# Two stages in one block with loads for the second under the first, and a basis summed on POOL, in a three-stage token mixer

## The chip, the cores and the metric

The kernel runs on one core of one Trainium2 chip. The core has five engines with instruction streams of their own: TensorE (PE in the profile; its weight loads are listed as PEld), VectorE (DVE), ScalarE (ACT), GpSimd (POOL), and SyncE (SP), which here only issues DMA transfers. The engines wait for each other through semaphores. The metric is the device time of one execution in microseconds (us), as the median of three runs.

## What is computed

The input x holds, for 16 batches, a complex 192 x 64 table. The reference makes three steps of it. The first, cut to what matters here:

```python
dtA = A * dt[:, None]
C = C * (jnp.exp(dtA) - 1.0) / A
ell = jnp.arange(L, dtype=jnp.float32)              # L = 512
V = jnp.exp(dtA[:, :, None] * ell)
K = 2.0 * jnp.einsum('chn,hnl->chl', C, V).real     # (16, 192, 512): 16 sequences of 192 rows
```

The second adds a retention layer to it: layernorm, projections q, k (512 wide), v and g (1024 wide), a rotary embedding on q and k, scores with a decay per head, an RMS norm of each head's output, a gate, and an output projection:

```python
scores = jnp.einsum('bihd,bjhd->bhij', q * scale, k) * D[None]
o = jnp.einsum('bhij,bjhd->bihd', scores, v)
o = o * rms * g_norm_weight
o = o * (g * jax.nn.sigmoid(g))
return o.reshape(B, T, H * DV) @ Wo
```

The third adds a causal softmax attention with 16 heads, whose keys and values are picked by a top-1 gate. The change does not touch the work of that step.

## The kernel before

The program is three blocks, one after the other: `block_p` (units), `block_q` (retention) and `block_f` (attention). Each block writes its rows to device memory (`h_tok`, `qk`, `v`, `g`, then `h2`), the next one reads them. At the end of a block all engines wait for each other and for the last stores, and only then does the next block begin.

**Units.** The 192 rows are cut into 24 units of 8 rows x 16 batches = 128 tokens. For each unit the first step's exponential is built from products of smaller tables. DVE makes two products, `pc` (real part of one digit times real part of the other) and `qs` (the imaginary counterparts), each 128 x 1024 (`build`, L523 and L525). POOL makes the moving operand `m` (`moving`, L644, L645, L650). TensorE's `spectrum` then adds the two products inside the matrix engine: for each of the 8 rows it runs one matmul with `pc` and one with `qs` as weights, both 64 columns wide, into the same accumulator (L698, L699), 16 matmuls in a unit.

After `spectrum(u+2)` a unit's rows are transposed to rows of tokens (`row_transposes`, L707), copied out by ACT (`h_evac`), their statistics taken (DVE L533, L536; POOL `scales`, L659 to L662), normalised (ACT L363), transposed back (`x_transposes`, L715), and split into a high and a low part (ACT `x_high` L370, DVE `x_low` L541). Six projections of 12 matmuls of 512 columns each follow (`project`, L724: q, k, v0, v1, g0, g1).

What stands in which slot is written out by hand in each engine's `slot(u)`. On TensorE slot u is: projection q of unit u, row transposes of u+1, projection k, spectrum of u+2, projections v0 and v1, transposes of x of u+1, projections g0 and g1. On POOL it is: `decay` (even u, L616), `scales(u+1)`, two `rope_add(u)` (L669), `corners` (every other unit, L626 to L632) and `moving(u+3)`. On DVE an even slot also holds `reduce` (L454 to L461) and `scale` (L512, L513) of the chunk two units on; ACT's part of that chunk is `trigonometry`. SP stores g of unit u-1, `h_tok` of u+1, and q/k and v of unit u (all L272).

In the first slots the six weight blocks are loaded through a buffer `stage` and split into `wr_high` (ACT `w_copy`, L313) and `wr_low` (DVE `split_weights`, L443), between the first units' work.

**Retention.** It goes over 8 pairs of batches of 384 tokens, in three tiles of 128 rows; tile 0 comes from units 0 to 15, the other tiles also need the last unit. SP's queue first loads q/k of pair 0 (`load_qk(0, t)`, L846 to L851, 1.5 MB), constants, v and g of pair 0 (1.5 MB each), the output weights `wo_raw` (2 MB), then q/k and v of pair 1. TensorE transposes q and k of pair 0 (L1098), computes the first scores (L1114), then transposes q and k of pair 1's tile 0 and runs the first `values` (L1130), in that order. ACT makes `wo_high` (L985) and DVE makes `wo_low` (`split_weights`, L1058, two instructions); on DVE these stand ahead of the first score masks (`masked`, L1002). In each slot DVE alternates masks with `gate_o` (L1013), which waits for POOL's norm (L1078 to L1081).

## Time and profile before

| what | value |
|---|---|
| median of three runs | 1482.92 us (1481.59 to 1484.98) |
| the profiled execution's own time | 1483.9 us |
| its span, first to last instruction | 1482.1 us |
| TensorE busy | 1322.8 us (89%), 8504 matmul records |
| DVE, ACT, POOL busy | 816.1, 595.5, 452.5 us |
| mean granted TensorE clock | 0.958 of full speed |

All rows shown are of that profiled execution. A row of the timeline gives the start, the time, the engine, the line, the operation with its tiles, how many instructions were merged into the row (x), and in brackets how long the engine had been idle before and who released it. A matmul of two f32 tiles is recorded as two instructions. Matmuls overlap in their records, so their spacing is read from the starts, not from the durations.

### The profile page before, as it was taken

What the parts mean: (1) busy time and instruction counts of PE and PEld (TensorE: products, weight loads), DVE (VectorE), ACT (ScalarE), POOL (GpSimd) and SP (SyncE); (2) the same over time, 40 slices, a digit from 0 to 9 for tenths busy, and PEclk for the clock granted to TensorE, in tenths of its full rate; (3) what the DMA queues carried; (4) which work ended last, traced back from release to release, by engine and by line L of the source; (5) the groups of instructions that cost most, each with busy time, mean ns of one, the idle gap of its engine ahead of it and who ended that gap; (6) DMA issues with size and microseconds to landing.
All of it is one profiled execution on the core that took longest, in us unless ns stands there. A gap on an engine that the chain in (4) does not pass through costs nothing. (4 is left out here: it accounts for less than half of the span.)

```text
span 1482.1 us, 23784 instructions
## 1 busy us (share of the span) xinstructions
PE 1322.8 (89%) x8504; PEld 1109.5 (75%) x8504; DVE 816.1 (55%) x1629; ACT 595.5 (40%) x1777; POOL 452.5 (31%) x696
## 2 busy tenths in 40 slices
PE   0799999999999995599999998489899998999997
PEld 0678888888888884478888886368788787878775
DVE  8656656655566321455555552345666656566566
ACT  3443333333334221333333321234546556454646
POOL 3555445544554310233333231021221203122121
PEclk9999999999999997799999999599999999999999
DMA  3222222222222225856655411354141423514040
GB/s 147 98 87 93 93 105 88 93 93 100 86 93 93 93 90 177 241 164 171 171 162 162 147 43 44 141 107 93 37 100 36 93 70 62 116 40 101 16 93 30
DMA packets 59525, 150.71 MB, mean 102 GB/s; under 512 B 7696, under 2 KB 24336, under 8 KB 57872
## 3 DMA queue, kind: packets, MB, share of 16 engines
q1 hardware_dynamic: 59408, 149.18, 34.0%
q8 instruction: 69, 1.13, 0.3%
q14 instruction: 48, 0.39, 0.1%
HBM read 67.37 MB, written 56.62 MB: 84 GB/s over the span
## 5 line engine op out<-in xcount | busy, mean ns | idle before, releaser
L724 PE MATMUL psum<-wr_high,x_high 128*128 128x512 f32 x576 | 234.1, 406 | 5.0 <-DVE x_low L541 5.0
L724 PE MATMUL psum<-wr_high,x_low 128*128 128x512 f32 x576 | 228.9, 397 | 0.0
L724 PE MATMUL psum<-wr_low,x_high 128*128 128x512 f32 x576 | 228.3, 396 | 0.0
L1466 ACT ACTIVATE probs<-psum,row_max 128x256 f32<-128x256 f32 (+1 forms) x384 | 165.1, 453 | 107.6 <-issue 75.2
L1716 POOL TENSOR_TENSOR picked_rows<-picked_rows 128x768 f32<-128x768 f32 (+1 forms) x64 | 61.0, 953 | 269.6 <-DVE picked_rows L1600 265.8
L724 PEld LDWEIGHTS psum<-wr_high,x_high 128*128 128x128 f32 x576 | 109.0, 189 | 28.6 <-DVE x_low L541 5.8
L724 PEld LDWEIGHTS psum<-wr_high,x_low 128*128 128x128 f32 x576 | 108.7, 189 | 25.9
L1618 DVE TENSOR_REDUCE row_max<-psum 128x2 f32<-128x512 f32 (+1 forms) x160 | 109.5, 684 | 31.8 <-PE psum L1821 31.8
L724 PEld LDWEIGHTS psum<-wr_low,x_high 128*128 128x128 f32 x576 | 109.1, 189 | 23.4
L937 ACT ACTIVATE square_scratch<-psum 128x128 f32<-128x128 f32 x192 | 50.7, 274 | 185.4 <-PE psum L1130 185.4
L698 PE MATMUL psum<-m,basis 128*128 128x64 f32 x384 | 76.8, 283 | 40.8 <-POOL m L650 40.8
L1013 DVE SCALAR_TENSOR_TENSOR gate_rows_q<-psum,rr,gate_rows_q 128x128 f32<-128x128 f32 x192 | 55.3, 344 | 91.7 <-POOL rr L1081 91.7
L1821 PE MATMUL psum<-k_stack_t,q_stack_t 128*128 128x256 f32 (+1 forms) x384 | 103.2, 365 | 0.0
L1832 PE MATMUL psum<-ident,probs 128*128 128x128 f32 x640 | 100.6, 281 | 1.5 <-ACT probs L1466 1.4
L698 PEld LDWEIGHTS psum<-m,basis 128*128 128x128 f32 x384 | 63.7, 203 | 42.7 <-issue 40.8
L1130 PEld LDWEIGHTS psum<-v_rows,s_t 128*128 128x128 f32 x640 | 81.2, 195 | 18.2 <-DVE s_t L1002 14.3
L1130 PE MATMUL psum<-v_rows,s_t 128*128 128x128 f32 x640 | 85.5, 282 | 9.3 <-DVE s_t L1002 9.3
L561 DVE SCALAR_TENSOR_TENSOR gate_rows<-gate_rows,psum 128x512 f32<-128x512 f32 x48 | 33.0, 687 | 102.4 <-ACT gate_rows L389 102.4
L1002 DVE SCALAR_TENSOR_TENSOR s_t<-psum,consts_r 128x256 f32<-128x256 f32 (+1 forms) x192 | 72.1, 432 | 25.7 <-PE psum L1114 25.7
L669 POOL TENSOR_TENSOR stage<-stage 128x512 f32<-128x512 f32 x48 | 81.0, 1701 | 14.9 <-DVE stage L556 14.9
L1832 PEld LDWEIGHTS psum<-ident,probs 128*128 128x128 f32 x640 | 77.6, 144 | 10.1 <-ACT probs L1466 2.4
L1466 ACT ACTIVATION_READ_ACCUMULATOR probs<-psum,row_max 128x1 f32 x384 | 84.5, 220 | 0.0
(200 smaller groups left out, 3027.5 us busy)
## 6 DMA issues: line engine op xcount, KB each, us to landing
qk<-stage SPq DMA_DIRECT2D x24, 512.0 KB, 2.6
v<-stage SPq DMA_DIRECT2D x24, 512.0 KB, 2.6
g<-gate_rows SPq DMA_DIRECT2D x24, 512.0 KB, 2.6
q_stack_t<-q_t_high SPq DMA_DIRECT2D x64, 192.0 KB, 4.2
q_stack_t<-q_t_low SPq DMA_DIRECT2D x64, 192.0 KB, 5.8
qk_rows<-qk SPq DMA_DIRECT2D x16, 512.0 KB, 5.5
v_rows<-v SPq DMA_DIRECT2D x16, 512.0 KB, 6.9
gate_rows_q<-g SPq DMA_DIRECT2D x16, 512.0 KB, 8.9
```

What stands on the lines that cost most here:

```text
L669: G.tensor_tensor(rqk[:, n], rt[:, n, 0], rt[:, n, 1], ALU.add).then_inc(rope_rows.sem, 1)
L698: nc.tensor.matmul(out, pc[:, f, h].rearrange("p x y -> p (x y)"), rhs, start=True, stop=False)
L724: last = nc.tensor.matmul(psum[:, PB[(6 * u[1] + n) % 4], :], x[:, q, k], ww[:, w, k, :], start=c == 0, stop=c == 3 * KC - 1)
L937: last = nc.scalar.activation(sqs[:, h % 2, t], psum[:, OB[h % 2], t * RV:(t + 1) * RV], ACT.Square, accum_out=ss[:, h % 2, t:t + 1])
L1002: last = V.scalar_tensor_tensor(st[:, h % 2, c], s_block(h, b), gk[:, kt, h:h + 1], mask[:, c], ALU.mult, ALU.mult)
L1013: last = V.scalar_tensor_tensor(y, psum[:, OB[h % 2], t * RV:(t + 1) * RV], rr[:, h % 2, 3, t:t + 1], y, ALU.mult, ALU.mult)
L1130: last = nc.tensor.matmul(psum[:, OB[h % 2], qt * RV:(qt + 1) * RV], st[:, h % 2, b * P:(b + 1) * P], v[:, i % 2, kt, hv], start=first, st ...
L1466: last = nc.scalar.activation(pr[:, g % 2, c], psum[:, SB[g % 3], c], ACT.Exp, scale=SCALE_F, bias=mx[:, g % 3, 1, x:x + 1], accum_out=dsu ...
L1618: V.reduce_max(mx[:, g % 3, 0, 0:nh], psum[:, SB[g % 3], :].rearrange("p (h n) -> p h n", h=nh), AX).then_inc(s_max.sem, 1)
L1716: return G.tensor_tensor(sel[:, x, :, 0:n], sel[:, x, :, 0:n], sel[:, x, :, n:2 * n], ALU.add)
L1821: last = mm(bank[:, x * nb * P:(x + 1) * nb * P], qsT[:, i % 2, h, t * P:(t + 1) * P], ksT[:, i % 2, k0:k0 + nb * P], start=False, stop=x ...
L1832: last = nc.tensor.transpose(psum[:, PTB[g % 2], x * P:(x + 1) * P], pr[:, g % 2, x * P:(x + 1) * P], ident[:, :])
```

## The change

There are four edits.

1. **Basis sum on POOL.** POOL gets a new step `basis_add(u)` at the end of its slot, after `moving(u+3)`: it waits for DVE's two products and adds `qs` to `pc`, one instruction over 128 x 1024. `spectrum` waits for it (semaphore `basis_summed`) and runs 8 matmuls instead of 16.
2. **One block.** Units and retention share one block: each engine goes from its last slot of the units into retention. Retention's buffers are laid over those of the units, so single waits on the last unit (`last_unit`) stand where one of its buffers or accumulators is reused.
3. **First loads under the last unit.** SP issues, in the last unit's slot and ahead of that unit's q/k and v stores, tile 0 of q/k, v and g of pair 0, the constants and `wo_raw` (`prefetch`). The other tiles of pair 0 follow when the stores that they need have landed.
4. **Weight split later.** DVE's two `split_weights` of the output projection stand in retention's slot 0 after the gates of heads 2 and 4, instead of ahead of the first mask. The accumulator banks of retention get other numbers.

```diff
+    def prefetch(sp):
+
+        for s in (*qk_in, *v_in, *g_in, *h_in, *stored):
+            s.prime(sp)
+        units["filtered"](sp)
+        load_qk(sp, 0, 0)
+        load_v(sp, 0, 0)
+        load_g(sp, 0, 0)
+        sp.dma_start(cr[:, :], d["consts_r"]).then_inc(const_in, 16)
+        sp.dma_start(gnorm_t[:, 0:1], d["g_norm"]).then_inc(const_in, 16)
+        for n in range(NW):
+            sp.dma_start(raw[:, n], d["w_f"][n].rearrange("p k f -> p (k f)")).then_inc(w_in[n], 16)
...
+        def basis_add(u):
+            f = u[1] % 2
+            pool.wait_ge(v_ready.sem, v_ready.of(u, 1))
+            flat = lambda x: x.rearrange("p h y x -> p (h y x)")
+            G.tensor_tensor(flat(pc[:, f]), flat(pc[:, f]), flat(qs[:, f]), ALU.add).then_inc(basis_sum.sem, 1)
...
             def spectrum(u):
                 f = u[1] % 2
-                pe.wait_ge(v_ready.sem, v_ready.of(u, 1))
+            pe.wait_ge(basis_sum.sem, basis_sum.of(u, 1))
...
-                    nc.tensor.matmul(out, pc[:, f, h].rearrange("p x y -> p (x y)"), rhs, start=True, stop=False)
-                    last = nc.tensor.matmul(out, qs[:, f, h].rearrange("p x y -> p (x y)"), rhs, start=False, stop=True)
+                last = nc.tensor.matmul(out, pc[:, f, h].rearrange("p x y -> p (x y)"), rhs, start=True, stop=True)
...
-            for t in range(NT):
-                load_qk(0, t)
-            sp.dma_start(cr[:, :], d["consts_r"]).then_inc(const_in, 16)
...
-            load_v(0)
-            load_g(0)
...
+        units["qk_stored"](sp)
+        load_qk(sp, 0, 1)
+        load_qk(sp, 0, 2)
+        units["v_stored"](sp)
+        load_v(sp, 0, 1)
+        load_v(sp, 0, 2)
+        units["g_stored"](sp)
+        load_g(sp, 0, 1)
+        load_g(sp, 0, 2)
+        units["h_stored"](sp)
...
+                elif m < HG - 1:
+                    split_weights(m - 1)
```

How the instructions stand now is shown at three places. The first is POOL in an odd slot of the units, before: the norm scales' last step, the two rope sums, the moving operand, and the next slot's scales.

```order
L662 TENSOR_TENSOR rs_p<-rs_p 128x1 [waits pool_chain_n]
L669 TENSOR_TENSOR stage<-stage 128x512 [waits qk_stored,rope_products]
L669 TENSOR_TENSOR stage<-stage 128x512 [waits rope_products]
L644 TENSOR_TENSOR mt<-cin,xy 128x512 [waits m_ready]
L645 TENSOR_TENSOR mt<-cin,xy 128x512
L650 TENSOR_TENSOR m<-mt 128x512 [waits k_summed,m_chain]
L659 TENSOR_TENSOR rs_p<-mv_p,small_p 128x1 [waits x_rows_normed,mean_var]
```

And the same place of the changed kernel:

```order
L682 TENSOR_TENSOR stage<-stage 128x512 [waits qk_stored,rope_products]
L682 TENSOR_TENSOR stage<-stage 128x512 [waits rope_products]
L651 TENSOR_TENSOR mt<-cin,xy 128x512 [waits m_ready]
L652 TENSOR_TENSOR mt<-cin,xy 128x512
L657 TENSOR_TENSOR m<-mt 128x512 [waits k_summed,m_chain]
L663 TENSOR_TENSOR basis<-basis 128x1024 [waits basis_products]
L672 TENSOR_TENSOR rs_p<-mv_p,small_p 128x1 [waits x_rows_normed,mean_var]
```

One instruction, the sum over 128 x 1024, stands behind the moving operand and ahead of the next slot's scales. The second place is SP's queue where the units end, before: the last unit's stores, the branch that waits for them all, the meeting of the engines, and the first loads.

```order
L272 DMA g<-gate_rows 128x1024 [waits gate_ready]
L272 DMA qk<-stage 128x1024 [waits rope_rows_ready]
L272 DMA v<-stage 128x1024 [waits v_evacuated]
L272 DMA g<-gate_rows 128x1024 [waits gate_ready]
L240 UNCONDITIONAL_BRANCH [waits v_stored,qk_stored,g_stored,h_stored1,h_stored0]
L837 UNCONDITIONAL_BRANCH [waits barrier_Pool_Activation_PE_DVE_SP_release]
L849 DMA qk_rows<-qk 128x1024
L846 DMA qk_rows<-qk 64x1024
L847 DMA qk_rows<-qk 64x1024
L851 DMA qk_rows<-qk 128x1024
L905 DMA consts_r<-in_consts_r 128x712
```

And of the changed kernel, from the store of g of the last unit but one to the first load that waits for a store:

```order
L285 DMA g<-gate_rows 128x1024 [waits gate_ready]
L882 DMA qk_rows<-qk 128x1024 [waits k_summed]
L882 DMA v_rows_even<-v 128x1024
L882 DMA gate_rows_even<-g 128x1024
L914 DMA consts_r<-in_consts_r 128x712
L915 DMA g_norm<-in_g_norm 128x1
L917 DMA wo_raw<-in_w_f 128x2048 x2
L285 DMA qk<-stage 128x1024 [waits rope_rows_ready]
L285 DMA v<-stage 128x1024 [waits v_evacuated]
L285 DMA g<-gate_rows 128x1024 [waits gate_ready]
L879 DMA qk_rows<-qk 64x1024 [waits qk_stored]
L880 DMA qk_rows<-qk 64x1024
```

Seven transfers have moved ahead of the last unit's three stores, and the meeting is gone. The rest follows in the order q/k, v, g of pair 0, then q/k of pair 1, as before. The third place is DVE where retention begins, before:

```order
L561 SCALAR_TENSOR_TENSOR gate_rows<-gate_rows,psum 128x512 [waits tanh_ready] x2
L240 UNCONDITIONAL_BRANCH
L989 UNCONDITIONAL_BRANCH [waits barrier_Pool_Activation_PE_DVE_SP_release]
L1058 SCALAR_TENSOR_TENSOR wo_low<-wo_raw,g_norm,wo_high 128x2048 [waits wo_high_ready,const_in_q]
L1058 SCALAR_TENSOR_TENSOR wo_low<-wo_raw,g_norm,wo_high 128x2048 [waits wo_high_ready]
L1002 SCALAR_TENSOR_TENSOR s_t<-psum,consts_r 128x256 [waits o_summed,scores_summed]
```

And of the changed kernel, in slot 0 where the first of the two splits now stands (the gates of head 1, the mask of head 3, the gates of head 2, the split, the mask of head 4):

```order
L1072 SCALAR_TENSOR_TENSOR gate_rows_even<-psum,rr,gate_rows_even 128x128 [waits o_norm_ready]
L1072 SCALAR_TENSOR_TENSOR gate_rows_even<-psum,rr,gate_rows_even 128x128 x2
L1061 SCALAR_TENSOR_TENSOR s_t<-psum,consts_r 128x256 [waits o_summed,scores_summed]
L1061 SCALAR_TENSOR_TENSOR s_t<-psum,consts_r 128x256
L1061 SCALAR_TENSOR_TENSOR s_t<-psum,consts_r 128x128
L1072 SCALAR_TENSOR_TENSOR gate_rows_even<-psum,rr,gate_rows_even 128x128 [waits o_norm_ready]
L1072 SCALAR_TENSOR_TENSOR gate_rows_even<-psum,rr,gate_rows_even 128x128 x2
L1089 SCALAR_TENSOR_TENSOR wo_low<-wo_raw,g_norm,wo_high 128x2048 [waits wo_high_ready]
L1061 SCALAR_TENSOR_TENSOR s_t<-psum,consts_r 128x256 [waits o_summed,scores_summed]
```

The splits no longer stand ahead of the first mask; each stands between a gate and the next mask.

## Rows read from the trace of the kernel before

**Rows 1.** Stage table, 100 us of the units: busy time of each engine.

```profile
100.00:200.00 100.00, 100.00 (x519) 83.72 (x518) 52.82 (x80) 35.22 (x58) 47.97 (x60) 1.00 0.25 96
```

**Rows 2.** TensorE timeline through one unit in the steady part.

```profile
389.64 0.60 PE L707 MATMUL psum<-ident,h_t 128*128 128x128 f32 x4
...
392.86 0.33 PE L698 MATMUL psum<-m,basis 128*128 128x64 f32 x2
...
396.35 0.48 PE L724 MATMUL psum<-wr_high,x_high 128*128 128x512 f32 x1
...
410.87 0.60 PE L707 MATMUL psum<-ident,h_t 128*128 128x128 f32 x4
```

**Rows 3.** POOL timeline through two units in the steady part.

```profile
400.50 1.06 POOL L645 TENSOR_TENSOR mt<-cin,xy 128x512 f32<-128x512 f32 x1
...
414.32 0.19 POOL L659 TENSOR_TENSOR rs_p<-mv_p,small_p 128x1 f32<-128x1 f32 x1 [10.48 <-DVE mv_p L536]
...
422.24 1.55 POOL L650 TENSOR_TENSOR m<-mt 128x512 f32<-128x512 f32 x1
```

**Rows 4.** DVE timeline in the same two units.

```profile
395.51 2.28 DVE L525 TENSOR_TENSOR basis<-q,sin_cos 128x1024 f32<-128x1024 f32 x1
...
422.56 1.71 DVE L513 TENSOR_TENSOR sin_cos<-sin_cos,mag 128x448 f32<-128x448 f32 x1
424.59 0.69 DVE L541 TENSOR_TENSOR x_low<-psum,x_high 128x512 fp32r<-128x512 f32 x1 [0.32 <-ACT x_high L370]
```

**Rows 5.** DVE timeline in the first 80 us: one operation of `reduce` twice.

```profile
39.45 1.57 DVE L458 SCALAR_TENSOR_TENSOR ang<-turn,ang 128x448 f32<-128x448 f32 x1
...
69.57 0.63 DVE L458 SCALAR_TENSOR_TENSOR ang<-turn,ang 128x448 f32<-128x448 f32 x1
```

**Rows 6.** TensorE timeline in the first 90 us, its waits after the first projection's start.

```profile
61.94 0.80 PE L724 MATMUL psum<-wr_high,x_high 128*128 128x512 f32 x1 [2.94 <-DVE x_low L541]
...
81.14 0.66 PE L715 MATMUL psum<-ident,x_rows 128*128 128x128 f32 x4 [0.96 <-ACT x_rows L363]
...
89.46 0.50 PE L724 MATMUL psum<-wr_high,x_high 128*128 128x512 f32 x1 [2.06 <-DVE x_low L541]
```

**Rows 7.** TensorE timeline from the units' last matmul into retention.

```profile
569.70 0.40 PE L724 MATMUL psum<-wr_high,x_low 128*128 128x512 f32 x1
580.03 1.97 PE L1098 MATMUL psum<-ident,qk_rows 128*128 128x128 f32 x8 [9.93 <-DMA qk_rows<-qk]
...
587.23 1.36 PE L1114 MATMUL psum<-q_t,k_t 64*128 64x128 f32 x12 [0.78 <-ACT k_t L927]
604.08 1.94 PE L1098 MATMUL psum<-ident,qk_rows 128*128 128x128 f32 x8 [15.49 <-DMA qk_rows<-qk]
607.15 4.23 PE L1130 MATMUL psum<-v_rows,s_t 128*128 128x128 f32 x20 [1.13 <-DVE s_t L1002]
```

**Rows 8.** DVE timeline where retention begins.

```profile
601.07 2.35 DVE L1058 SCALAR_TENSOR_TENSOR wo_low<-wo_raw,g_norm,wo_high 128x2048 fp32r<-128x2048 f32 x1 [29.62 <-ACT wo_high L985]
603.70 2.35 DVE L1058 SCALAR_TENSOR_TENSOR wo_low<-wo_raw,g_norm,wo_high 128x2048 fp32r<-128x2048 f32 x1 [0.28 <-ACT wo_high L985]
...
618.65 0.87 DVE L1013 SCALAR_TENSOR_TENSOR gate_rows_q<-psum,rr,gate_rows_q 128x128 f32<-128x128 f32 x3 [2.32 <-POOL rr L1081]
619.54 1.13 DVE L1002 SCALAR_TENSOR_TENSOR s_t<-psum,consts_r 128x256 f32<-128x256 f32 x3
```

**Rows 9.** SP's queue around the end of the units: times at which transfers were issued.

```profile
554.67 0.32 SPq L272 DMA_DIRECT2D g<-gate_rows  x1
...
571.48 0.32 SPq L272 DMA_DIRECT2D g<-gate_rows  x1
575.34 0.32 SPq L849 DMA_DIRECT2D qk_rows<-qk  x1
...
584.59 0.45 SPq L849 DMA_DIRECT2D qk_rows<-qk  x1
```

**Rows 10.** Stage table, 575.3 to 604 us; the last three columns are granted clock, DMA share, GB/s.

```profile
575.30:604.00 28.70, 7.09 (x36) 5.73 (x36) 2.65 (x2) 7.59 (x8) 0.00 (x0) 0.56 0.97 292
```

More of the change, by code:

```diff
@@ L14 @@
 from contextlib import ExitStack
+from dataclasses import dataclass
 import numpy as np
@@ L1244, in block_f @@
-def block_f(nc, sem, sb, psum, ident, d):
+                    wo(i - 1, m - 1, 1)
+                if here:
+                    values(i, 2 * m + 1)
+                if ahead:
+                    if back and m == 1:
+                        pe.wait_ge(y_low.sem, y_low.at(i - 1, 6))
+                    pe.wait_ge(qkt_out.sem, qkt_out.at(i + 1, 1 if m == 1 else 4))
+                    qk_transposes(i + 1, m, 1)
+            if here:
+                scores(i, 3)
+            if back:
+                wo(i - 1, 2, 0)
```

2741 lines of the change are left out of this document (1395 added, 1346 removed).

## The prediction

> **What bounds the kernel now.** I read the stage table first. In the units TensorE has no idle time (100.00 us of 100) while POOL is busy for 47.97 us and DVE for 52.82 us [rows 1]. So there a matmul less is time less, as long as nothing else becomes late, and work added to POOL is free as long as it stays within POOL's idle time. Then I read TensorE's timeline through one unit. It repeats every 21.23 us (389.64 to 410.87 us), and `spectrum` takes 3.49 us of it (392.86 to 396.35 us) for 16 matmuls, 0.218 us each [rows 2]. That leaves the places where TensorE does wait: the first 90 us, where each wait names another engine [rows 6], and the passage into retention. Between the units' last matmul (its end taken at 570.1 us, call it T) and the first `values` at 607.15 us lie 37.05 us, in which TensorE waits 9.93 us and then 15.49 us for q/k rows from memory [rows 7]. The queue of transfers is full there: DMA share 0.97 at 292 GB/s, while TensorE is busy for 7.09 of 28.70 us at a granted clock of 0.56 [rows 10]. The attention stage keeps its instructions and is not touched.
>
> **Edit 1, steady part.** `spectrum` keeps 8 of its 16 matmuls: 8 x 0.218 = 1.745 us less in a unit, which becomes 19.49 us. There are 24 spectra; slot u does that of u+2, so slots 1 to 21 hold 21 of them in the part without waits. 21 x 1.745 = **36.6 us**. (If the 8 keep less overhead at their edges than the 16, it is up to 37.4.)
>
> What pays is POOL. No 128 x 1024 sum of POOL's is in the trace; the nearest row is its 128 x 512 product of 1.06 us when nothing holds it up [rows 3], so 2.1 us, and with the 1.55 us form of such an operation [rows 3] 3.1 us. POOL is idle for 10.48 us between the moving operand's slot and the next norm scales [rows 3], and the sum falls into that gap. Two slots now take 39.0 us, POOL's work in them 2 x 0.48 x 21.23 = 20.4 us plus 4.2 to 6.2. It is not the bound, and the sum for unit u+3 ends at the start of the next slot's projection of q, some 7 us ahead of the `spectrum` that waits for it. `moving` stands ahead of it, so `m` is not later. Queued behind it are `decay` and the scales, which wait for other things in the gap anyway. Price on the path: nothing; without the gap it would be 2.1 us a unit.
>
> The second way in which POOL's sum could cost is DVE. In the trace DVE's product over 128 x 1024 takes 2.28 us where POOL works, and `scale`'s second product 1.71 us, while the product ahead of `x_low`, which reads the accumulator, takes 0.69 us [rows 4]. So operations of DVE with two operands in SBUF wait for POOL's to end, the one with an accumulator does not show it. The Trainium skill says so too (SBUF — State Buffer, "Who interferes with whom"): a DVE instruction with two SBUF inputs and a GpSimd one that reads SBUF exclude each other for a whole instruction. By that rule the place to look at is an even unit, where POOL's `m` ends at 423.8 us and DVE's `scale` only then gets through; if POOL's sum went first, `x_low` would come 2.1 us later. `x_low` ends at 425.28 us; the q projection that needs it starts at 410.87 + 21.23 - 12 x 0.233 = 429.3 us, 1.745 us earlier in the changed kernel, at 427.55 us [rows 2, 4]. 427.4 is still in time, so either order costs nothing there.
>
> **Edit 1, first slots.** Here TensorE waits for others. The first projection at 61.94 us waits for `x_low`, slot 0's transposes at 81.14 us for ACT's normalised rows, slot 1's first matmul for `x_low` again [rows 6]: none of them waits for `spectrum`, so the three spectra up to slot 0 save nothing. And the chain to the first of these runs through DVE's `reduce`, whose operations already wait for POOL: 1.57 us against 0.63 us for the same one when POOL is idle [rows 5]. With POOL's sums of units 0 and 2 of 2.1 us each in its row there, I take one such sum less a little for the first (1.7 us) and 0.8 us for the second, whose splits DVE can partly do in its gaps: **2.5 us lost**, between 0 and 4.
>
> **Edits 2 and 3, the passage.** Before, the first loads were issued at 575.34 us, T + 5.2, and q/k of pair 1's tile 0, issued at 584.59 us, landed at 604.08 us [rows 7, 9]. `values` of pair 0 stands behind the transposes of that tile in TensorE's program, before and after. What decides is therefore when this load lands, and since the queue is full it is a matter of kilobytes: ahead of it and with it went 1536 (q/k) + 356 + 1536 (v) + 1536 (g) + 2048 (weights) + 512 = 7524 KB, in 28.74 us, 262 KB/us. After, the queue starts right behind the store of g of the last unit but one, issued at 554.67 us [rows 9], so at T - 15.1. The bytes are the same and the last unit's stores of q/k, v and g besides, 1536 KB: 9060 KB. At 262 KB/us that is 34.6 us, to T + 19.5; at the 292 GB/s of the full stretch [rows 10], 285 KB/us, 31.8 us, to T + 16.7. The single waits don't let the queue run empty: the store of g is issued 1.4 us behind T [rows 9] with the weights and two stores still in the queue. I take T + 19, nearer to the same loads. Then 1.94 us of transposes [rows 7] and `values` starts at T + 20.9 instead of T + 37.05: 16.1 us gained. The first transposes of pair 0 need tiles 1 and 2 of q/k: 3940 KB of prefetch, 1536 of stores and 1024 of their own are 6500 KB or 24.8 us, T + 9.7; two thirds of the 7.2 us that all three tiles took before the first scores (580.03 to 587.23 us [rows 7]) puts the scores at T + 14.5, so they are not the last to end. I keep the half clock for this stretch as before, since TensorE is idle from about T + 1 on again.
>
> **Edit 4.** Before, the two splits (2.35 us each) ended at 606.05 us, under the wait for the same load [rows 8], so moving them gains about 1 us that the next step already counts. In slot 0 DVE goes from a gate at 618.65 us, for which it waited, straight to the next mask at 619.54 us [rows 8], and TensorE's next `values` waits for that mask. A split between the two comes in full on the path, twice: 2 x 2.35 = **4.7 us lost** (3 to 6.5, since POOL's small norm operations may have to wait for it too). The passage is then 16.1 - 4.7 = **11.4 us** gained, between 7 and 18. Later loads follow with the same distance or more before their users.
>
> **Sum.** 36.6 - 2.5 + 11.4 = 45.5 us. The profiled execution's span of 1482.1 us becomes 1436.6. It took 1483.9 us itself, 1.0 above the median; against the median of 1482.92 us the forecast is 1437.4 us.
>
> **The rivals.**
> - *The passage gives nothing* (the stores and the prefetch share one full queue, the q/k rows land no earlier than edit 4 takes back): the queue holds 1536 KB more, 5.9 us, and could be slower for mixed directions. For the 11.4 us to vanish, the load would have to land at T + 30, at 200 KB/us, against 262 seen. 1482.9 - 34.1 = 1448.8 us. Chance 0.09.
> - *POOL's sum makes `x_low` or `decay` late in each even unit.* The slack is 2.3 us against 2.1; with a sum of 3.1 us [rows 3] it would be overrun by 0.8 us in 10 pairs, 8 us, and by 2 us if ACT's late copy joins. 1437.4 + 8 to 20: 1445 to 1457 us. Chance 0.08. The Trainium skill's GPSIMD Engine Reference ("Elementwise") speaks for it: it gives a two-input add of 2048 elements as 4497 ns on GpSimd and 2293 on VectorE and says to use the latter. By that figure the sum is an estimated 2.2 us, and the forecast stays.
> - *Both sums of the passage come out well* (rate 285 KB/us, or first scores' work hidden wholly, splits partly under a wait): 1430 us. Inside the main case's range.
> - *Slower: POOL becomes the bound of the units.* It would need more than 21.23 us of POOL a unit, so a sum of over 11 us on top of 10.2. Rows give 2.1 to 3.1. At 13 us the unit is 23.2 us: 21 x 2.0 = 42 us more, 1482.9 + 42 - 11.4 + 2.5 = 1516 us. It turns the sign only when the sum takes 11.5 us. Chance 0.02.
> - *Nothing of the saved matmuls comes through* (the wait goes to something that is just ready now): 1482.9 - 11.4 + 2.5 = 1474 us. Against it: every engine but TensorE has idle time in [rows 1]. Chance 0.03.
>
> **How the numbers follow.** The main case has 0.78 and alone 1428 to 1446 us: 37.4 + 18 - 0 = 55.4 us gained at best, 36 + 7 - 4 = 39 at worst, drawn in a little. With the first rival the range becomes 1428 to 1450 us, which leaves out about 0.15. A change within 0.2% (3 us) is about what a measurement can't tell from none: for it, gains of 45 would have to fall to 3, 0.01. Slower by more: 0.02. Faster: 0.97.
>
> **What the profile of the changed kernel would show.** Right: a unit's period of 19.5 us with `spectrum` at 1.75 us; POOL's sum at 2.1 to 2.4 us and no TensorE wait for it after the first slots; the first projection at 63 to 64 us; q/k of pair 1 landing 19 us behind the units' last matmul and `values` 21 us behind it; two splits of 2.35 us in slot 0, each followed by a mask 2.4 us later than before. Wrong: TensorE waiting for POOL's sum or for `x_low` in the steady part, a spectrum matmul that takes more than 0.22 us alone, a queue below 262 KB/us, or `values` released by something other than that load.

## The result, and the profile after

The changed kernel takes **1425.7 us** in the median of four runs (1419.7 to 1429.29). The kernel before, run beside it, takes 1483.79 us (1481.59 to 1484.98). The ratio is 0.9611, with a 95% interval of 0.9575 to 0.9647. That is some 57.7 us less. The forecast was 1437.4 us, with a range of 1428 to 1450 us. So the sign and most of the gain were right, and the time fell 2.3 us outside the range on the fast side. In four of the experiments below, and once in the kernel before beside them, a single run took over 1900 us; medians and ratios leave such a run out.

The profiled execution took 1429.29 us, the slowest of the four; its span is 1427.5 us, 54.6 us less than before.

The stage table for the same 100 us as [rows 1]: busy time of PE, PEld, DVE, ACT, POOL, then granted clock, DMA share, GB/s.

```profile
100.00:200.00 100.00, 100.00 (x501) 83.95 (x500) 62.26 (x91) 40.31 (x65) 68.46 (x73) 1.00 0.27 105
```

TensorE still has no idle time there. POOL went from 47.97 to 68.46 us and DVE from 52.82 to 62.26 us. Part of that is only that more units fit into 100 us (5.2 instead of 4.7): in a unit POOL is busy 13.1 us instead of 10.2, and DVE, whose work is the same, 11.9 instead of 11.2. The timeline of TensorE in the steady part, which answers to [rows 2]:

```profile
381.09 0.60 PE L719 MATMUL psum<-ident,h_t 128*128 128x128 f32 x4
384.31 1.89 PE L711 MATMUL psum<-m,basis 128*128 128x64 f32 x16
...
400.23 0.60 PE L719 MATMUL psum<-ident,h_t 128*128 128x128 f32 x4
403.44 1.89 PE L711 MATMUL psum<-m,basis 128*128 128x64 f32 x16
```

One unit is now 400.23 - 381.09 = **19.14 us**, against 21.23 before and 19.5 forecast. POOL in the steady part, 110 to 500 us, as groups (busy, mean ns of one, idle before):

```profile
L663 POOL TENSOR_TENSOR basis<-basis 128x1024 f32<-128x1024 f32 x19 | 48.7, 2561 | 0.0
```

The sum takes 2.56 us, somewhat more than the 2.1 to 2.4 us named. No TensorE row in the steady part has a wait, for it or for `x_low`. In the even slot around 394 us DVE's `scale` (392.89 us) went ahead of the sum (394.08 us, 2.78 us long), and `x_low` ended at 395.20 us, 2.3 us ahead of the projection that needs it (397.51 us). So the prediction's "either order costs nothing" isn't shown: with the sum first, 2.78 us would not have fitted into 2.3. In the first slots TensorE waits as in [rows 6], each time a little later:

```profile
63.14 0.80 PE L736 MATMUL psum<-wq_high,x_high 128*128 128x512 f32 x1 [4.18 <-DVE x_low L549]
82.83 1.12 PE L727 MATMUL psum<-ident,x_rows 128*128 128x128 f32 x4 [3.75 <-ACT x_rows L372]
91.16 0.50 PE L736 MATMUL psum<-wq_high,x_high 128*128 128x512 f32 x1 [0.90 <-DVE x_low L549]
```

Slot 1 starts at 91.16 instead of 89.46 us: 1.7 us lost. Why it is late, POOL's row and DVE's show (two timelines of the changed kernel):

```profile
40.40 2.71 POOL L663 TENSOR_TENSOR basis<-basis 128x1024 f32<-128x1024 f32 x1
...
66.48 4.37 POOL L663 TENSOR_TENSOR basis<-basis 128x1024 f32<-128x1024 f32 x1 [2.29 <-DVE basis L533]
```

```profile
40.95 2.65 DVE L467 SCALAR_TENSOR_TENSOR ang<-turn,ang 128x448 f32<-128x448 f32 x1
...
68.52 2.81 DVE L462 TENSOR_TENSOR ang<-w,consts_a 128x448 f32<-128x448 f32 x1
```

An operation of `reduce` that takes 0.6 us alone [rows 5] lasts 2.65 us when POOL's sum is under way beside it, and POOL's second sum lasts 4.37 us beside DVE. Where units and retention meet, TensorE's timeline answers to [rows 7]:

```profile
526.61 0.39 PE L736 MATMUL psum<-wg_high,x_low 128*128 128x512 f32 x1
526.84 1.03 PE L1158 MATMUL psum<-ident,qk_rows 128*128 128x128 f32 x8
533.99 3.74 PE L1158 MATMUL psum<-ident,qk_rows 128*128 128x128 f32 x16 [6.11 <-DMA qk_rows<-qk]
538.51 2.51 PE L1177 MATMUL psum<-q_t,k_t 64*128 64x128 f32 x12 [0.78 <-ACT k_t L977]
544.07 1.94 PE L1158 MATMUL psum<-ident,qk_rows 128*128 128x128 f32 x8 [3.05 <-DMA qk_rows<-qk]
545.80 4.30 PE L1197 MATMUL psum<-v_rows_even,s_t 128*128 128x128 f32 x20
550.03 1.35 PE L1177 MATMUL psum<-q_t,k_t 64*128 64x128 f32 x12
...
577.02 1.35 PE L1177 MATMUL psum<-q_t,k_t 64*128 64x128 f32 x11
```

T, the end of the units' last matmul, is from here on its start and one distance to the next: 526.61 + 0.23 = 526.84 us, and 569.93 us before. (The prediction took 570.1 us, so its times behind T for the kernel before are 0.2 us smaller.) The load of q/k of pair 1 lands at T + 17.2 (forecast T + 19), and `values` starts at T + 19.0 (forecast T + 20.9, before T + 37.2). It is released by that load, as forecast. 577.02 us are the first scores of slot 1. SP's queue, which answers to [rows 9]:

```profile
512.06 0.32 SPq L285 DMA_DIRECT2D g<-gate_rows  x1
513.23 0.32 SPq L882 DMA_DIRECT2D qk_rows<-qk  x1
...
515.80 1.14 SPq L917 DMA_DIRECT2D wo_raw<-in_w_f  x2
...
528.39 0.32 SPq L285 DMA_DIRECT2D g<-gate_rows  x1
528.75 0.54 SPq L879 DMA_DIRECT2D qk_rows<-qk  x1
...
534.29 0.35 SPq L882 DMA_DIRECT2D qk_rows<-qk  x1
```

The first load goes out at T - 13.6 instead of T + 5.4. The 9060 KB of the prediction's count came in the 30.8 us up to T + 17.2, so at 294 KB/us, faster than the two rates of the forecast (262 and 285); but they started 1.5 us later than its T - 15.1. The rate varies: in the ten profiles of this study with the passage of before, the same 7524 KB took 25.2 to 31.3 us (299 to 240 KB/us), and the 28.7 us that the prediction read are one of the slower ones; in the six with the early loads the 9060 KB took 30.7 to 32.5 us. DVE in slot 0, which answers to [rows 8]:

```profile
558.13 0.87 DVE L1072 SCALAR_TENSOR_TENSOR gate_rows_even<-psum,rr,gate_rows_even 128x128 f32<-128x128 f32 x3 [3.33 <-POOL rr L1142]
558.92 2.35 DVE L1089 SCALAR_TENSOR_TENSOR wo_low<-wo_raw,g_norm,wo_high 128x2048 fp32r<-128x2048 f32 x1
561.18 1.13 DVE L1061 SCALAR_TENSOR_TENSOR s_t<-psum,consts_r 128x256 f32<-128x256 f32 x3
```

The split stands between gate and mask, and TensorE's `values` after it waits 3.02 us for this mask.

Cut at three moments that every profile has, the two profiled executions compare like this (us):

| stretch | before | after | difference | forecast |
|---|---|---|---|---|
| start to T | 569.9 | 526.8 | -43.1 | -34.1 |
| T to slot 1's first scores | 63.2 | 50.2 | -13.0 | -11.4 |
| from there to retention's last matmul with `wo` | 291.6 | 289.0 | -2.5 | 0 |
| from there to the end (the attention) | 557.5 | 561.4 | +3.9 | 0 |

The last line is no effect of the change. The attention has the same instructions in all kernels of this study, and in the other fifteen profiled executions it took 548.8 to 558.5 us. What is left to explain is the first line, 9 us more than forecast.

The starts of the matmuls give the lead. I took the mean distance between two successive 512-column matmuls from TensorE's timeline (starts are given to 0.01 us, so the mean is over some 1300 pairs in the units). In the units it was 0.2332 us before and is **0.2288 us** after; in retention 0.2333 and 0.2272 up to 820 us (0.2278 with its last slot); in the attention 0.2332 in both. The two rows of each pair below are 28 distances apart, first before, then after: 6.53 us and 6.39 us, or 0.2332 and 0.2282 us a matmul. The forecast had kept 0.233.

```profile
466.40 0.39 PE L724 MATMUL psum<-wr_low,x_high 128*128 128x512 f32 x1
...
472.93 0.39 PE L724 MATMUL psum<-wr_high,x_low 128*128 128x512 f32 x1
```

```profile
392.25 0.40 PE L736 MATMUL psum<-wg_low,x_high 128*128 128x512 f32 x1
...
398.64 0.39 PE L736 MATMUL psum<-wq_high,x_low 128*128 128x512 f32 x1
```

72 such matmuls a unit at 4.4 ns less are 0.32 us, and 24 units make 7.6 us. Nothing in the change says that a matmul takes less. But since retention's buffers had to fit over the units', nearly every tile got another address in SBUF.

### The profile page after: what moved, and what is told of

Same layout as the page of the kernel before. It is cut to its first block and busy times, and to the rows that moved or that the text cites. A ratio compares the mean times of both kernels' runs of the same rounds, so it can differ in the third digit from the quotient of the medians.

```text
span 1427.5 us, 23033 instructions
## 1 busy us (share of the span) xinstructions
PE 1272.5 (89%) x8120; PEld 1069.5 (75%) x8120; DVE 818.5 (57%) x1629; ACT 593.6 (42%) x1777; POOL 518.0 (36%) x720
## 5 line engine op out<-in xcount | busy, mean ns | idle before, releaser
L1806 POOL TENSOR_TENSOR h_rows<-h_rows,y_normed 128x512 f32<-128x512 f32 x24 | 30.6, 1277 | 168.3 <-DVE y_normed L1706 168.3
L1139 POOL TENSOR_TENSOR rr<-ss,consts_r 128x3 f32<-128x3 f32 x64 | 14.1, 221 | 212.2 <-ACT square_scratch L987 211.0
L711 PE MATMUL psum<-m,basis 128*128 128x64 f32 x384 | 48.8, 284 | 43.2 <-POOL basis L663 43.2
L1220 PE MATMUL psum<-wo_high,y_high 128*128 128x512 f32 x192 | 80.3, 418 | 1.7 <-issue 1.7
L736 PE MATMUL psum<-wg_high,x_high 128*128 128x512 f32 x192 | 77.7, 405 | 0.0
L1862 PE MATMUL psum<-wf_high,x_high 128*128 128x512 f32 x192 | 76.1, 397 | 1.3 <-DVE picked_rows L1669 1.3
L736 PE MATMUL psum<-wv_high,x_high 128*128 128x512 f32 x192 | 77.1, 401 | 0.0
L1220 PE MATMUL psum<-wo_high,y_low 128*128 128x512 f32 x192 | 75.8, 395 | 0.0
L1220 PE MATMUL psum<-wo_low,y_high 128*128 128x512 f32 x192 | 75.8, 395 | 0.0
L1862 PE MATMUL psum<-wf_low,x_high 128*128 128x512 f32 x192 | 75.8, 395 | 0.0
```

The costliest lines, as they stand in the source:

```text
L711: last = nc.tensor.matmul(out, pc[:, f, h].rearrange("p x y -> p (x y)"), rhs, start=True, stop=True)
L736: last = nc.tensor.matmul(psum[:, PB[(6 * u[1] + n) % 4], :], x[:, q, k], ww[w][:, k, :], start=c == 0, stop=c == 3 * KC - 1)
L1220: last = nc.tensor.matmul(psum[:, WB, :], y[:, h, ts], w[:, h, :], start=n == 0, stop=n == 3 * RH - 1)
L1862: last = mm(psum[:, bank, :], x[:, k, ts], ww[:, w, k, :], start=n == 0, stop=n == 3 * KC - 1)
```

## The experiments

Each kernel was run beside the kernel before on the same chip; the medians of before were 1478.9 to 1483.8 us. "Theory" is first that of the tiles' places: edits 1 to 4 are worth what they are in the prediction, and the rest comes from the matmuls' distance.

### Edit 1 alone

```diff
+            def basis_add(u):
+                f = u[1] % 2
+                pool.wait_ge(v_ready.sem, v_ready.of(u, 1))
+                G.tensor_tensor(flat(pc[:, f]), flat(pc[:, f]), flat(qs[:, f]), ALU.add).then_inc(basis_sum.sem, 1)
...
-                pe.wait_ge(v_ready.sem, v_ready.of(u, 1))
+                pe.wait_ge(basis_sum.sem, basis_sum.of(u, 1))
...
-                    nc.tensor.matmul(out, pc[:, f, h]..., rhs, start=True, stop=False)
-                    last = nc.tensor.matmul(out, qs[:, f, h]..., rhs, start=False, stop=True)
+                    last = nc.tensor.matmul(out, pc[:, f, h]..., rhs, start=True, stop=True)
```

> The kernel before with the basis sum on POOL and 8 spectrum matmuls alone; blocks, buffers and their places are as before. The changed kernel's unit repeats in 19.1 us instead of the 19.49 forecast, and its 512-column matmuls of the units start every 0.2288 us instead of every 0.2332. Placement theory (the spacing comes from where the tiles lie in SBUF): here the spacing stays 0.233 us, the unit is 19.5 us, and the total is 35 us below the kernel before (36.6 less 1.7 in the first slots), about 1449 us. Rival (the shorter spacing comes with the basis edit, since TensorE does less in between or POOL works more): spacing 0.229 us, unit 19.1 us, 43 us below, about 1441 us.

Measured: 1442.6 us (1438.77 to 1446.41), ratio 0.974 (0.9715 to 0.9764). The distance in the units stays at 0.2332 us. T is 534.2 us. Its timeline at a `spectrum`:

```profile
466.88 1.89 PE L706 MATMUL psum<-m,basis 128*128 128x64 f32 x16
486.32 1.89 PE L706 MATMUL psum<-m,basis 128*128 128x64 f32 x16
```

The unit is 19.44 us, 1.79 less than 21.23, where the forecast had 1.745. 21 x 1.79 = 37.6, less the 1.8 us by which slot 1 starts late (91.28 us), is 35.8, and T moved by 35.7. So edit 1 is worth 35.7 us, 1.6 more than the forecast's 34.1. The median lies nearer to the rival's 1441 than to the theory's 1449, but both were reckoned from 1484 us. The kernel before beside it had a median of 1479.9 us, and against that the gain is 37.3 us, where the theory had 35 and the rival 43. The profile decides it: the distance did not change and T moved by what the saved matmuls give. The other 6 us of this profile's span lie behind T, in the passage and the attention, which this kernel shares with the kernel before and which vary by as much (below). The missing 7.4 us up to T = 526.8 are not edit 1's.

### Edits 2 to 4 alone

The changed kernel without `basis_add`: `spectrum` has its 16 matmuls again and waits for DVE.

> The changed kernel with 16 spectrum matmuls and no sum on POOL; one block, prefetch, split order and the new places of the buffers stay. Passage: 12.8 us below the kernel before from there alone, as read from the changed kernel's trace (slot 1's first scores 50.2 us behind the units' last matmul against 63.0). Placement theory: the spacing of the units' 512-column matmuls is 0.229 us here too, a unit takes 20.8 to 20.9 us, 8 to 10 us more come from there, total about 1461 us. Rival (spacing comes with the basis edit): spacing 0.233 us, unit 21.23 us, total about 1471 us.

Measured: 1460.49 us (1458.21 to 1463.06), ratio 0.9859 (0.9837 to 0.9881). Distance 0.2287 us in the units and 0.2272 in retention. T is 564.1 us, 5.8 us earlier than before with all 16 matmuls in each `spectrum`, and slot 1's first scores stand at T + 50.2. The total is the theory's 1461 us and not the rival's 1471. The two halves add up: 0.974 x 0.9859 = 0.9603 against 0.9611.

### The tiles' places alone

The kernel before with the SBUF layout of the changed one in the units, retention's untouched:

```diff
-    w_hi = sb("wr_high", [P, NP, KC, D], F32R)
-    w_lo = sb("wr_low", [P, NP, KC, D], F32R)
+    names = ("wq", "wk", "wv0", "wv1", "wg0", "wg1")
+    w_pairs = [(sb(n + "_high", [P, KC, D], F32R), sb(n + "_low", [P, KC, D], F32R)) for n in names]
```

and the smaller tiles declared in the changed kernel's order.

> The kernel before with nothing changed but the places of the units' tiles in SBUF: the order of the changed kernel, each weight block a high and a low tile side by side, x_high and x_low behind g4. Placement theory: spacing 0.229 us in the units and 0.233 us in retention, whose tiles did not move; total 7 to 9 us below the kernel before, about 1475 us. Rival (places do not matter): 0.233 us in both, no difference, 1484 us.

Measured: 1469.48 us, ratio 0.9928 (0.9903 to 0.9953). Not one instruction is added or taken away, and T moved from 569.9 to 562.8 us. The distance is 0.2287 us in the units and still 0.2334 in retention, whose tiles did not move. So places alone give 7 us.

### Both splits in the gap ahead of `values`

```diff
             if here:
                 masked(i, 1)
+            if i == 0:
+                split_weights(0)
+                split_weights(1)
...
-                elif m < HG - 1:
-                    split_weights(m - 1)
```

> The changed kernel with both weight splits of retention's slot 0 right behind the mask of head 1, where DVE is idle for 7.78 us in the changed kernel's trace, instead of behind the gates of heads 2 and 4. My reckoning of edit 4 (each split there lies in full on the path, 2.35 us): 4.7 us or a little more faster than the changed kernel, and values of heads 4 and 6 wait 2.3 us less each; with less idle time TensorE's half-clock stretches in slot 0 may go as well, then 6 us. Rival (the splits are hidden behind the norm chain anyway): no difference to the changed kernel.

Measured: 1414.96 us (1412.02 to 1417.86), ratio 0.9551 (0.9528 to 0.9574). DVE does both splits in one piece while TensorE waits for q/k:

```profile
541.24 2.18 DVE L1061 SCALAR_TENSOR_TENSOR s_t<-psum,consts_r 128x256 f32<-128x256 f32 x6 [12.74 <-PE psum L1178]
543.33 4.61 DVE L1089 SCALAR_TENSOR_TENSOR wo_low<-wo_raw,g_norm,wo_high 128x2048 fp32r<-128x2048 f32 x2
```

Slot 1's first scores come at T + 44.6 (571.59 us) instead of T + 50.2: 5.6 us for two splits of 2.35 us. Two stage rows of this kernel:

```profile
550.00:560.00 10.00, 6.59 (x57) 5.64 (x54) 6.54 (x22) 3.29 (x19) 5.21 (x14) 1.00 1.02 302
560.00:570.00 10.00, 7.80 (x64) 6.64 (x62) 5.34 (x17) 5.47 (x28) 4.63 (x14) 1.00 0.29 72
```

and the same two of the changed kernel:

```profile
550.00:560.00 10.00, 7.68 (x53) 6.93 (x52) 5.59 (x16) 3.70 (x20) 5.00 (x13) 0.83 0.87 268
560.00:570.00 10.00, 6.30 (x40) 5.86 (x40) 7.58 (x15) 2.82 (x14) 5.63 (x8) 0.83 0.27 79
```

The granted clock (third number from the end) is 1.00 with the splits in the gap and 0.83 with the splits behind the gates. In the timelines the 5.6 us fall into two halves. The waits for the two masks behind a split are 3.02 and 2.17 us against 1.24 us each, 2.7 us more. The rest, 2.8 us, are two stretches at 1.2 GHz, from 553.05 to 557.99 us and from 562.36 to 567.31 us, of 4.94 and 4.95 us against 3.56 us at the full clock. The second of them in the changed kernel, and the same work with the splits in the gap:

```profile
562.36 1.54 PE L1197 MATMUL psum<-v_rows_even,s_t 128*128 128x128 f32 x10 [3.02 <-DVE s_t L1061]
...
564.55 2.34 PE L1197 MATMUL psum<-v_rows_even,s_t 128*128 128x128 f32 x10
```

```profile
559.25 1.38 PE L1198 MATMUL psum<-v_rows_even,s_t 128*128 128x128 f32 x10 [1.24 <-DVE s_t L1061]
...
561.06 1.38 PE L1198 MATMUL psum<-v_rows_even,s_t 128*128 128x128 f32 x10
```

The first of the two stretches stands ahead of the first split (558.92 us), so that split can't have caused it. A stretch like the second follows nearly every late mask: in the four profiles with this passage and the splits behind the gates, seven of the eight waits for such a mask are followed by a stretch at the lower clock; in the two with the splits in the gap none of the four waits of 1.24 us is. A stretch like the first comes in three of these six profiles, one of them with the splits in the gap.

### The loads behind the last unit

```diff
-            if u == (0, NU - 1):
+            if u == (0, NU):
                 prefetch(sp)
```

> The changed kernel with the first loads of the retention put behind the last unit's last store instead of ahead of the last unit; the engines still don't meet, the sum of the basis products and the two splits stay. Theory (the transfers set the passage): one tile each of q/k, values and gates, the constants and both halves of the raw output weights now queue behind the units instead of under them; at the 295 KB/us of the passage these 3.9 MB take 13 us, of which the gap behind the last unit swallowed some already: q/k of pair 1 lands 9 to 11 us later, measured from the units' last matmul (T + 27 in place of T + 17), the values follow, and the kernel is 8 to 11 us slower than the changed one, about 1433. Rival (the meeting of the engines was the cost, the prefetch little): under 3 us slower than the changed one.

Measured: 1438.57 us (1434.55 to 1439.59), ratio 0.9725 (0.9704 to 0.9747), against 1423.88 for the changed kernel in the same batch: 14.7 us slower, more than either theory said. TensorE's waits:

```profile
534.03 1.94 PE L1158 MATMUL psum<-ident,qk_rows 128*128 128x128 f32 x8 [6.94 <-DMA qk_rows<-qk]
546.65 1.94 PE L1158 MATMUL psum<-ident,qk_rows 128*128 128x128 f32 x8 [10.68 <-DMA qk_rows<-qk]
...
558.29 1.94 PE L1158 MATMUL psum<-ident,qk_rows 128*128 128x128 f32 x8 [4.18 <-DMA qk_rows<-qk]
```

T is 526.9 us as in the changed kernel; q/k of pair 1 lands at T + 31.4 instead of T + 17.2, and slot 1's first scores at T + 63.9 instead of T + 50.2. I had let the gap swallow part of the 13 us of transfers; it swallowed none, since the queue is full from there to the load that decides. From the first load (529.65 us) to that one the 7524 KB of the kernel before took 28.6 us, against 28.7 there. What this kernel still has over the kernel before, the first load at T + 2.7 instead of T + 5.4, is what leaving out the meeting of the engines gives: under 3 us.

The same stretch, T to slot 1's first scores, over all profiles:

| kernels | us |
|---|---|
| ten with the passage of before | 60.5 to 66.7, eight of them 60.5 to 62.0 |
| four with the passage of the changed kernel | 50.2, 51.0, 50.2, 51.4 |
| loads late, splits behind the gates | 63.9 |
| loads early, both splits in the gap | 44.6, 45.7 |

### The changed kernel again

> The changed kernel itself once more, on the chip of these experiments, as the yardstick: 1422 to 1427 against the 1480 of the kernel before, a ratio of 0.961. If it comes out at 0.957 or lower, part of the advantage that the version with the splits in the gap showed (0.955) was the chip's and not the splits'.

Measured: 1423.88 us (1419.36 to 1424.53), ratio 0.9618 (0.9597 to 0.964). So the version with the splits in the gap is ahead by 0.0067 of 1480, 10 us. The profiles show 5 to 7 us of it in the passage; the rest is within what the two intervals leave open.

### Which tile it is

First the weights alone in turn, high and low, with all else in place, and then all else moved and the weights in place:

```diff
-    w_hi = sb("wr_high", [P, NP, KC, D], F32R)
-    w_lo = sb("wr_low", [P, NP, KC, D], F32R)
+    w_pairs = [(sb(n + "_high", [P, KC, D], F32R), sb(n + "_low", [P, KC, D], F32R)) for n in names]
```

> The kernel before with the weight tiles of the units lying high, low, high, low; every other tile stays. With the small tiles moved instead (x_high and x_low among them) the spacing fell to 0.2287 us. Theory (the place of x_high and x_low sets it): spacing 0.233, no difference from before. Rival (any change of the two operands' distance does it): 0.229 and 5 to 10 us faster.

> The other half: weight tiles as before, all the smaller tiles of the units placed as in the changed kernel, x_high and x_low at bytes 178048 and 182144 of a partition instead of 197632 and 201728. Theory (the weights' places set it): spacing 0.233 and no difference from before. Rival (the place of x): 0.229 and 7 to 10 us faster. If both this one and the paired weights lie between, the distance between the two operands counts.

Measured: the weights in turn 1480.75 us, ratio 0.9988 (0.9969 to 1.0007), distance 0.2332 us, no difference. The rest moved: 1473.82 us, ratio 0.9961 (0.9938 to 0.9984), distance 0.2287 us, T 562.9 us. My theory of the weights' order is wrong; it is the place of `x_high` and `x_low`. Of the 7 us that this profile shows at T the runs show 5; their interval holds both.

### Pads

From here the kernel before gets only pads, and the three stages are read apart, each with its own tile: x in the units, y in retention, x2 in the attention.

```diff
+    sb("pad_x", [P, 224])
     xhi = sb("x_high", [P, 2, KC, P], F32R)
...
+    sb("pad_y", [P, 584])
     yhi = sb("y_high", [P, RH, TP], F32R)
...
+    sb("pad_x2", [P, 240])
```

> The kernel before with three pads: 896 bytes ahead of x_high (which then starts at byte 198528 of a partition), 2336 ahead of y_high (165760) and 960 ahead of x2_high (108416), so that each starts 1920 bytes past a multiple of 4096, as x_high does in the changed kernel. Theory (the offset of the loaded tile within a block of 4096 bytes sets the spacing of the 512-column matmuls): 0.227 to 0.229 us in the units, the retention and the attention alike, and 12 to 20 us faster than before. Rival (what counts is the region, or another tile that moved along): spacing 0.233 in all three and no difference.

> The kernel before with three other pads: x_high at 198144 (1536 past a multiple of 4096), y_high at 164864 and x2_high at 107520 (both 1024 past one, as x_high of the kernel before). Theory of the offset: y and x2 stay at 0.233; what x shows at 1536 is open and tells how fine the rule is. Rival (any move helps): all three at 0.229.

> The kernel before with three further pads: x_high at 198272 (640 past a multiple of 1024, as the first weight tile), y_high at 164096 (256 past), x2_high at 108288 (768 past). So far 896 past gave 0.2287 to 0.2295 and 0, 512, 608 and 960 gave 0.232 to 0.233. Theory of a narrow rule (only near 896): all three at 0.232 to 0.233, no difference from before. Rival (a band): y or x2 at under 0.231 us, by which the kernel gains up to 3 us.

Measured: the first 1470.07 us, ratio 0.9911 (0.9884 to 0.9938); the second 1476.97 us, 0.9966 (0.995 to 0.9982); the third 1472.22 us, 0.9931 (0.9907 to 0.9956). The second gained 0.3% with no stage below 232 ns and T no earlier than before (571.4 us; the four kernels without the closer distance in the units and with all 16 matmuls have 569.9 to 571.4), so a ratio of this size alone says nothing of the places; the distances and T do. The first brought all three stages under 0.230 us. That three pads with no work in them give 12 us is the plainest form of the finding. The third refuted my narrow rule: x at 640 past a multiple of 1024 is as fast as at 896. What 640 and 896 have in common is 128 past a multiple of 256, and so do all weight tiles of these kernels, which start at byte 17024. Whether the loaded tile's own offset counts or its offset against the weights', the next pair was to tell.

### The offset itself, or the offset against the weights

```diff
+    sb("pad_wp", [P, 32])
     w_hi = sb("wr_high", [P, NP, KC, D], F32R)
```

(the same ahead of `wo_high` and `wf_high`), and pads ahead of x, y and x2 that put them at multiples of 256 in the first, at 128 past one in the second.

> The kernel before with pads that put the weight tiles of all three stages (wr, wo, wf) at byte 17152, a multiple of 256, and x_high, y_high and x2_high, with their low parts, on multiples of 256 too. Theory (the offset of the loaded tile against the weight tile counts, equal offsets are fast): spacing 0.227 to 0.2295 us in all three stages. Rival (the loaded tile has to start 128 past a multiple of 256, whatever the weights do): 0.232 to 0.233 in all three, no difference from before.

> The same weights at byte 17152, with x_high, y_high and x2_high at 128 past a multiple of 256. Theory (equal offsets are fast): 0.232 to 0.233 in all three stages, no difference from before. Rival (the loaded tile's own offset): 0.227 to 0.2295 in all three, and 8 to 13 us faster than before.

Measured: both on multiples of 256, 1468.2 us (1467.12 to 1468.94), ratio 0.9897 (0.9869 to 0.9924); only the weights on one, 1477.3 us, ratio 0.9971 (0.9945 to 0.9997). Two successive units of the first and of the second, in TensorE's timelines:

```profile
470.28 0.60 PE L709 MATMUL psum<-ident,h_t 128*128 128x128 f32 x4
491.21 0.60 PE L709 MATMUL psum<-ident,h_t 128*128 128x128 f32 x4
```

```profile
475.00 0.60 PE L708 MATMUL psum<-ident,h_t 128*128 128x128 f32 x4
496.17 0.60 PE L708 MATMUL psum<-ident,h_t 128*128 128x128 f32 x4
```

20.93 us a unit against 21.17. All of it in one table. TensorE streams the weight tiles (`wr`, `wo`, `wf`) past a block of x, y or x2 that was loaded before; "128/0" means that the weight tile starts 128 bytes past a multiple of 256 and the loaded tile on one. The number is the mean distance of the 512-column matmuls in ns.

| kernel | units | retention | attention |
|---|---|---|---|
| before | 128/0: 233.2 | 128/96: 233.3 | 128/192: 233.2 |
| changed | 128/128: 228.8 | 128/128: 227.2 | 128/192: 233.2 |
| pads, first | 128/128: 228.7 | 128/128: 229.7 | 128/128: 228.4 |
| pads, second | 128/0: 233.2 | 128/0: 232.2 | 128/0: 232.2 |
| pads, third | 128/128: 228.7 | 128/0: 232.1 | 128/0: 232.4 |
| both on 256 | 0/0: 228.7 | 0/0: 229.7 | 0/0: 228.6 |
| weights on 256 | 0/128: 232.3 | 0/128: 232.5 | 0/128: 232.3 |

Where the two operands have the same offset within 256 bytes the distance is 227 to 230 ns, where they differ 232 to 233, in twenty-one of twenty-one stages, and the rival of the loaded tile's own offset falls. The unequal pairs tried are 96, 128 and 192 bytes apart; a smaller difference was not tried.

### The miss taken back

The changed kernel with 128 bytes of pad ahead of `x_high` and of `y_high`:

```diff
+    sb("pad_x", [P, 32])
     xhi = sb("x_high", [P, 2, KC, P], F32R)
...
+    sb("pad_y", [P, 32])
     yhi = sb("y_high", [P, RH, TP], F32R)
```

> The changed kernel with two pads of 128 bytes, ahead of x_high and ahead of y_high, which put them on multiples of 256; nothing else. Theory (the places of these tiles explain the miss): spacing 0.232 to 0.233 in units and retention, the units' last matmul 7 us later (534 in place of 527), 8 to 11 us slower than the changed kernel: 1432 to 1435, a ratio of 0.968, inside the range that was predicted. Rival (another part of the change brought the closer spacing too): under 3 us slower than the changed kernel.

Measured: 1433.0 us (1429.46 to 1437.35), ratio 0.966 (0.9632 to 0.9688); distance 0.2327 us in the units and 0.2318 in retention; T 533.4 us. The 256 bytes of pad cost some 6 us by the ratios (0.966 against 0.9618), 6.5 at T in the profiles. This kernel, with all four edits, lies in the range that was forecast.

### The fastest version

The splits in the gap, and 960 bytes of pad ahead of x2.

> The changed kernel with the two splits in the gap ahead of the values (as in the version that gave 0.955) and, in the attention, a pad of 960 bytes ahead of x2_high, which puts it at byte 108416, 1920 past a multiple of 4096. Theory (matmuls at the closer spacing shorten the attention too): some 540 matmuls of 512 columns there, 4.5 ns less each, 2 us at most: 1410 to 1414. Rival (the attention doesn't wait for these matmuls): spacing 0.2285 there, and the same time as without the pad, a ratio of 0.955.

Measured: 1414.17 us (1412.02 to 1416.62), ratio 0.9544 (0.9521 to 0.9568); distance 0.2283 us in the attention. That is the same as without the pad (0.9551). The runs can't tell the theory (529 matmuls at 4.9 ns less, at most 2.6 us) from the rival (nothing): the two intervals are each some 7 us wide. The profiles don't settle it either. The attention took 553.7 us here and 550.3 and 556.0 us in the two other kernels with the shorter distance, and 548.8 to 561.4 us in those without. In the profile of the kernel before, these matmuls do stand on the chain of work that ended last, with 21% of the stretch behind 930 us, so the rival's reason isn't shown. Splits in the gap, with or without this pad, is the fastest kernel of the study, 10 us ahead of the changed one.

## Why the prediction was right and where it was wrong

- **"21 x 1.745 = 36.6 us": the step that failed.** Its mechanism was right, its size was not, and nearly all of the excess is in what it left out. The row said 16 matmuls from 392.86 to 396.35 us, and half of them went. The saving was 1.79 us a unit, so 37.6 us; the bracket with 37.4 was close. But the units gained 7.4 us more, since the term took the other 72 matmuls of a unit as unchanged at 0.233 us. They came at 0.2288, because `x_high` and `x_low` had moved to the same offset within 256 bytes as the weights. Shown by the places alone (-7.1 us at T), by pads (-7.0 us at T), and by taking it back (+6.5 us): with the two tiles off by 128 bytes the changed kernel took 1433.0 us, inside the range.
- **"POOL's sum costs nothing on the path": right.** 2.56 us instead of 2.1, no wait behind it in the steady part. That it did not matter which of DVE's `scale` and POOL's sum goes first was reckoned with 2.1 us; at 2.56 to 2.78 us against 2.3 us of room it is the order seen in the trace that held, and the other was not tried. By the Trainium skill (GPSIMD Engine Reference, "Elementwise") the estimate was 2.2 us; the shortest in the trace is 2.34 us.
- **"2.5 us lost" in the first slots: right in kind, 1.7 to 1.8.** Two operations of `reduce` took 2.65 and 2.81 us under POOL's sum instead of some 0.6 us alone, the mechanism that [rows 5] had shown.
- **The passage, "11.4 us gained": right, 13.0 in the profiled pair.** Over all profiles it is the difference between 60.5 to 62 and 50.2 to 51.4 us, some 10 to 11. Inside it two terms were off and cancelled in part. The load landed at T + 17.2, at the fast end of T + 16.7 to 19.5, since the queue moved 294 KB/us instead of 262, a rate that varies by as much between profiles: 18.3 us gained at `values` instead of 16.1. The splits, "4.7 us lost", cost 5.6 in one pair of profiles and 5.3 in the other (51.0 against 45.7). That is not two full splits: the waits grew by 2.7 us in the first pair, and stretches at the lower clock, which the term did not have, make up the rest.
- **"The attention is not touched": right.** Retention's later slots gained 2.5 us, which no step had: 576 matmuls with `wo` at 5.5 to 6.1 ns less are 3.2 to 3.5 us. Pads alone brought this stretch from 291.6 to 288.3 us; taking the places back in the changed kernel gave 289.9 us against 288.2 and 289.0, so there only a part of it came back.
- **The sum.** 35.7 + 7.4 + 13.0 + 2.5 = 58.6 us against 57.7 measured and 45.5 forecast. Of the 13.1 us between, 7.4 are the tiles' places in the units and up to 2.5 those in retention. The sum leaves out the attention, which ran 3.9 us longer in this one profile.
- **The range** was too narrow because every bound in it was on a cost that the diff names. Its upper end is also no sum of its terms: 39 us gained at worst is 1443.9 us, and the text has 1446. That a changed layout changes the speed of untouched matmuls was in no rival.

The rivals: the passage gave something; POOL's sum delayed neither `x_low` nor `decay`; POOL did not become the bound.

What stays open is why. The Trainium skill (SBUF — State Buffer, "Who interferes with whom") gives TensorE one read port for the moving operand and an independent one for weight loads, and says of the engines' contention that it never waits on anyone. It says nothing on where the two tiles start; the runs show 4.5 ns a matmul. Open too is why y at 128/128 gave 227.2 ns in the changed kernel and 229.7 with pads alone; there other tiles and the accumulator banks differ as well.

## What to carry to other kernels

When a change moves buffers, read the distance of the matmuls that it does not touch, before and after, and put the operand that is loaded and the one that streams at the same offset within 256 bytes: here a pad of 896 bytes was worth 7 us of 570 in the units, where TensorE has no idle time; in the attention no gain could be told from the noise. When a queue is full, count its kilobytes up to the load that decides; work that an engine can do while that load is under way belongs there and not behind it, the more so since seven of eight waits for such late work were followed here by a stretch at half the clock.

## What the hardware showed that was not expected

- 512-column matmuls with a weight load each come every 227 to 230 ns where both tiles have the same start modulo 256 bytes, and every 232 to 233 ns otherwise (table above). In the kernel before, the distances alternate by the place in a projection's group of twelve: 227 to 229 ns, then 237 to 238 ns; in the changed kernel they lie between 224 and 232.
- Two splits of 2.35 us behind the gates cost 5.3 to 5.6 us. In the profiled pair some half of it is waiting and half is TensorE's clock at 1.2 GHz; the clock fell after seven of the eight waits for a mask behind a split, and after none of the four waits for the same masks with the splits in the gap.
- One and the same row of loads, 7524 KB through the full queue, took 25.2 to 31.3 us in ten profiles. A forecast that takes its rate from one of them carries that error.
- The attention's share of the span varied from 548.8 to 561.4 us over seventeen executions of the same instructions. So a difference of 5 us between two profiled spans says little unless it is cut at moments like T.
